# A decoder layer with two attentions: other filler slots, reciprocals copied by ScalarE, an earlier weight split and a deferred normalisation

## The reference

```python
x = layernorm(x + self_attention(x, Wq, Wk, Wv, Wo))          # causal, 16 heads of 32, 4 key/value heads
x = layernorm(x + cross_attention(x, ctx, Wq, Wkv, Wout))      # causal, 16 heads, latent context of 128
x = layernorm(x + ffn(x))                                      # gate, then 2 layers of two matrix products each
```

## Time and profile before

| | |
|---|---|
| Runs, us | 988.43, 987.88, 986.71; median 987.88 |
| Profiled execution, us | 984.96, span 983.1, mean granted TensorE clock 0.971 |
| Busy share of the span | PE 91%, PEld 75%, DVE 69%, ACT 56%, POOL 51% |
| Turn 0 begins (first scores) | 20.8 us |
| Turns 1 to 6 (loop) | 46.5 to 231.3 us |
| Turn 7 | 231.3 to 276.9 us |
| Turn 8 | 276.9 to 332.3 us |
| Turns 9 to 14 | 332.3 to 596.1 us |
| Turn 15 and flush | 596.1 to 653.3 us, where the feed-forward phase has its first TensorE work |

### The profile page before, as it was taken

One profiled execution on the slowest core, in us unless ns is written; L12 is line 12 of the kernel. 1 busy time (PEld: TensorE's weight loads), 2 busy tenths in 40 slices (PEclk: granted clock), 3 DMA queues, 4 the chain that ended last, 5 costly groups with the idle time before them and its releaser, 6 DMA issues. The chain is left out here.

```text
span 983.1 us, 19518 instructions
## 1 busy us (share of the span) xinstructions
PE 892.4 (91%) x5892; PEld 735.8 (75%) x5892; DVE 677.2 (69%) x2055; ACT 550.1 (56%) x1674; POOL 496.7 (51%) x793
## 2 busy tenths in 40 slices
PE   4999999998898899999999998669899999999893
PEld 4888888887776678778777877457678778778672
DVE  4687778786785777777876766426757657667557
ACT  4756556664664566565755556427564464564461
POOL 0445555455755345454645432610665565566466
PEclk9999999999899999999999999879999999999997
DMA  4644243444665556574654636344002001001001
GB/s 155 222 144 158 98 160 128 160 160 143 210 205 145 168 159 194 166 225 121 188 170 138 181 110 197 132 167 155 0 1 85 3 1 55 32 1 40 4 0 43
DMA packets 79075, 118.53 MB, mean 121 GB/s; under 512 B 7920, under 2 KB 41744, under 8 KB 78224
## 3 DMA queue, kind: packets, MB, share of 16 engines
q1 hardware_dynamic: 78992, 117.52, 37.2%
HBM read 58.76 MB, written 17.83 MB: 78 GB/s over the span
## 5 line engine op out<-in xcount | busy, mean ns | idle before, releaser
L920 ACT ACTIVATE prob<-bank,nmax 128x128 f32<-128x128 f32 (+1 forms) x512 | 209.9, 431 | 38.5 <-DVE nmax L1049 36.9
L161 PE MATMUL bank<-w_ffn,hT 128*128 128x512 f32 x768 | 192.8, 402 | 0.0
L1049 DVE CUSTOM_DVE_ANT_0 bank<-bank,mask 128x128 f32<-128x128 f32 (+1 forms) x512 | 167.6, 383 | 4.0 <-PE bank L1225 3.7
L161 PEld LDWEIGHTS bank<-w_ffn,hT 128*128 128x128 f32 x768 | 141.5, 189 | 30.9
L161 PE MATMUL bank<-xT,w_att 128*128 128x256 f32 x864 | 124.1, 298 | 22.0 <-DVE w_att L961 10.3
L161 PEld LDWEIGHTS bank<-xT,w_att 128*128 128x128 f32 x864 | 115.4, 201 | 31.7 <-DVE xT L1037 9.7
L777 POOL TENSOR_TENSOR zone<-raw,zone 128x256 fp32r<-128x256 f32 x128 | 95.2, 776 | 65.8 <-ACT zone L900 65.8
L1237 PE MATMUL bank<-ident,prob 128*128 128x128 f32 x768 | 119.7, 279 | 4.5 <-ACT probT L933 4.4
L933 ACT ACTIVATE probT<-bank 128x512 f32<-128x512 f32 x97 | 58.3, 603 | 92.7 <-PE bank L1261 91.6
L920 ACT ACTIVATION_READ_ACCUMULATOR prob<-bank,nmax 128x1 f32 x512 | 110.0, 215 | 0.0
L1547 ACT ACTIVATE ht<-bank,cols 128x128 f32<-128x128 f32 x192 | 72.3, 457 | 66.0 <-PE bank L1715 66.0
(11 more groups left out here) (118 smaller groups left out, 1518.7 us busy)
## 6 DMA issues: line engine op xcount, KB each, us to landing
q<-stage SPq DMA_DIRECT2D x192, 128.0 KB, 2.2
k<-kstage SPq DMA_DIRECT2D x48, 256.0 KB, 3.5
x<-xres SPq DMA_DIRECT2D x16, 512.0 KB, 4.0
raw<-in_ent_wT SPq DMA_DIRECT2D x32, 256.0 KB, 3.8
raw<-in_ent_pw SPq DMA_DIRECT2D x32, 256.0 KB, 4.1
raw<-in_xT SPq DMA_DIRECT2D x8, 512.0 KB, 3.6
raw<-in_path_w SPq DMA_DIRECT2D x8, 512.0 KB, 3.7
xres<-in_x SPq DMA_DIRECT2D x8, 512.0 KB, 4.9
```

The lines of the kernel that those rows point to most:

```text
L161: ins = t.matmul(out, lhs(a, k), rhs(b, k), start=first and n == 0 and m == 0, stop=last and n == len(kts) - 1 and m == 2, skip_group_chec ...
L920: ins = s.activation(prob[:, u, c * width:(c + 1) * width], banks[u][:, c * width:(c + 1) * width], ACT.Exp, scale=-1.0, bias=nmax[:, i % ...
L1049: ins = v.tensor_tensor_reduce(scored, scored, mask[:, S - width:S], scale=-1.0, scalar=3e38, op0=ALU.add, op1=ALU.min, accum_out=nmax[:, ...
```

## The change

Five things change. First, the slots of a self turn: sv 1 moves from slot 1 to slot 0, wo 0 from slot 2 to slot 1. In turn 8 wo 0 and wo 1 move forward within their slots, in turn 15 cq 3, wout 0 and wout 1 move one slot ahead. Second, the copy rT goes from VectorE to ScalarE, behind the exponentials of unit 0; VectorE's product o now stands behind the maxima of unit 1. Third, in turn 7 the weights of the cross attention are split in slots 0, 1 and 2 (1, 4 and 1 pieces), where they were in slots 0, 1, 2 and 3 (1, 2, 2, 1). Fourth, their pieces are loaded earlier (two already in turn 0), for which they take other places in the parking area. Fifth, a slot's last normalisation stands behind the following step on VectorE, except in the last slot of a turn. GpSimd's split of the next input (`split_x`) goes ahead of the slot's fillers.

```diff
         if own == "self":
-            out[0] += [("sv", 0), ("sq", 2)]
-            out[1] += [("sv", 1), ("sq", 3)]
+            out[0] += [("sv", 0), ("sq", 2), ("sv", 1)]
+            out[1] += [("sq", 3)]
+            if wo:
+                out[1] += [(wo, 0)]
             if after == "self":
+                out[2] += [("sk", 0), ("sq", 0)]
                 if wo:
-                    out[2] += [(wo, 0)]
                     out[3] += [(wo, 1)]
-                out[2] += [("sk", 0), ("sq", 0)]
                 out[3] += [("sq", 1)]
             else:
                 out[1] += [("x1t", 0), ("x1t", 1)]
-                out[2] += [("wo", 0), ("ck", 0), ("cq", 0), ("sp", 0), ("sp", 1)]
+                out[2] += [("ck", 0), ("cq", 0), ("sp", 0), ("sp", 1)]
                 out[3] += [("wo", 1), ("cq", 1), ("ck", 1), ("sp", 2)]
         elif own == "cross" and after:
             out[0] += [U, U, ("cq", 2), U]
             if wo == "wo":
-                out[1] += [U, ("cq", 3), U, ("cv", 0), ("cv", 1), ("x1t", 0), ("x1t", 1), U, ("wo", 0)]
-                out[2] += [U, ("ck", 0), U, ("cq", 0), ("wo", 1)]
+                out[1] += [U, ("cq", 3), U, ("wo", 0), ("cv", 0), ("cv", 1), ("x1t", 0), U, ("x1t", 1)]
+                out[2] += [U, ("wo", 1), ("ck", 0), U, ("cq", 0)]
...
         elif own == "cross":
-            out[0] += [("cq", 2)]
-            out[1] += [("cq", 3), ("cv", 0), ("cv", 1), ("gs", 0), ("gs", 1)]
-            out[2] += [("wout", 0), ("gs", 2), ("gs", 3)]
-            out[3] += [("wout", 1), ("gs", 4), ("gs", 5)]
+            out[0] += [("cq", 2), ("cq", 3)]
+            out[1] += [("cv", 0), ("cv", 1), ("wout", 0), ("gs", 0), ("gs", 1)]
+            out[2] += [("wout", 1), ("gs", 2), ("gs", 3)]
+            out[3] += [("gs", 4), ("gs", 5)]
...
-            return {(0, False): (OUTPUTS, C_KEYS), (1, False): (C_KEYS, C_KEYS + 2), (2, True): (C_KEYS + 2, C_QUERIES),
-                    (3, True): (C_QUERIES, C_VALUES)}.get((i, early), (0, 0))
+            return {(0, False): (OUTPUTS, C_KEYS), (1, False): (C_KEYS, C_QUERIES), (2, False): (C_QUERIES, C_VALUES)}.get((i, early), (0, 0))
...
                 if t is last_self:
-                    load_piece(0)
+                    wait_alone(q, s_wlo, OUTPUTS, s_passed)
+                    load_piece(2)
+                    load_piece(3)
...
                     if i == 2 and t is first:
+                        load_piece(0)
+                        load_piece(1)
...
                         load_path(t)
-                        for n in range(1, 4):
-                            load_piece(n)
+                        wait_alone(q, s_pbm, 2, s_passed)
+                        load_piece(4)
+                        load_piece(5)
...
                         if t.scored(i):
                             exponentials(u)
+                        if u == 0 and t.closed(i):
+                            n = t.groups(i - 2)
+                            s.wait_ge(s_O, n)
+                            if t.before or i > 2:
+                                s.wait_ge(s_o, t.groups(i - 3))
+                            s.activation(rT[:, i % 2, :], banks[O_BANK][:, S:2 * S], ACT.Copy).then_inc(s_rT, 1)
...
                     n = t.groups(i)
-                    v.wait_ge(s_O, n)
                     bank = banks[O_BANK]
-                    v.tensor_copy(rT[:, i % 2, :], bank[:, S:2 * S]).then_inc(s_rT, 1)
                     v.wait_ge(s_rT, n)
...
-                        if u == 0 and t.closed(i):
+                        if u == 1 and t.closed(i):
                             output(i - 2)
...
+                ready = None
                 for i in range(t.steps()):
                     step(i)
+                    if ready:
+                        normalise(*ready)
+                        ready = None
                     weights(*split_at(t, i, True))
-                    ready = None
...
-                    if ready:
+                    if ready and i == t.steps() - 1:
                         normalise(*ready)
```

More of the change, by code:

```diff
@@ L473, in attention_phase @@
     parked = zone_raw[:, 2 * 4 * D:2 * 4 * D + PARKED * D].rearrange("p (n d) -> p n d", n=PARKED)
+    PARKING = [2, 3, 0, 1, 4, 5]
     modb = zone_raw[:, 3 * 4 * D:4 * 4 * D].rearrange("p (n d) -> p n d", n=NL * NP)
@@ L479, in piece_home @@
         if n < PARKED:
-            return parked[:, n, :], s_wring[n], 16
+            return parked[:, PARKING[n], :], s_wring[n], 16
         return x1b[:, n % 2, :], s_wring[PARKED + n % 2], 16 * ((n - PARKED) // 2 + 1)
@@ L664, in between @@
                             q.dma_start(A["fd"][l, 1][:, KT, :], acc[:, NP * l, :]).then_inc(s_pbst, 16)
-                        for n in range(4, PARKED):
-                            load_piece(n)
                         wait_alone(q, s_xs, B, s_passed)
@@ L821, in body @@
                         path_bias(i)
+                    if i == 1 and t.after == "self":
+                        split_x()
                     for name in t.fillers(i):
@@ L828, in body @@
                             gate_lo(name[1])
-                    if i == 1 and t.after == "self":
-                        split_x()
                     if i == 1 and t.after == "cross":
```

## The result

| | before | after |
|---|---|---|
| Runs, us | median 987.88 (986.71 to 991.15, 5 runs) | median 1046.02 (1042.08 to 1052.38, 5 runs) |
| Ratio, 95% interval | | 1.0593 [1.0553, 1.0633] |
| Profiled execution: span, mean granted clock | 983.1, 0.971 | 1050.6, 0.937 |

The change makes the kernel 5.9% slower. The forecast was 1048 us.

The account below looks back on a forecast made before the run. TensorE's work was taken to bound loop and cross turns, with waits in turns 7 and 8. Terms summing to +62.6 us on the profiled 984.96 gave 1047.5, forecast as 1048 us, range 1000 to 1068.

Parts of the forecast that it names:

- (a): Slot 0 of a loop turn: sv 1 waits at least 2.0 us for ScalarE to copy sv 0.
- (b): Each step: rT on ScalarE lengthens the chain; sv 0 is free 6.2 us after the first maxima, against 5.2.
- m: Loop turn: time from its start to VectorE's first maxima, which would grow from 3.0 to 6.0 us.
- The clock: Loop turns: the low clock after a wait of 6 us adds 2.5 us per turn, bounds 0 and 4.
- (c): Slot 1 of a loop turn: wo 0 waits 1.65 us for GpSimd's split of the previous turn's last group.
- the extra DMA in turn 0 (0.5 MB) is hidden: Turn 0: the extra 0.5 MB load costs nothing, since what stands behind it is not needed for 4 us.
- the first: Loop turns: waits alone, m near 3 us, wait 3.0, clock up; turn 33.9 us, kernel about 1015; chance 0.21.
- The faster case: Evened slots hide VectorE if sv 0 is copied within 6.2 us of a turn's start; about 966 us; chance 0.12.

Follow-up runs that it names:

- experiment 6: The changed kernel with wo 0 of the self turns back in slot 2: 1042.2 us, ratio 1.0572 to the kernel before.
- experiment 7: The changed kernel with sv 1 and wo 0 in their old slots and rT back on VectorE: 976.2 us, ratio 0.9884 to before.
- experiment 4: The kernel before with rT copied by ScalarE and o behind the maxima of unit 1: 1020.7 us, ratio 1.0337.
- experiment 3: The kernel before with sv 1 moved to slot 0 of the self turns alone: 999.8 us, ratio 1.012.
- experiment 5: The changed kernel with sv 1 back in slot 1 and rT back on VectorE, wo 0 staying in slot 1: 986.6 us, ratio 0.9983 to before.
- experiment 1: The changed kernel with sv 1 back in slot 1 of the self turns: 1021.8 us, ratio 1.037 to before.
- experiment 8: The changed kernel with GpSimd's path work cut to 32 of 512 columns: 1027.7 us, ratio 1.0411 to before.
- experiment 9: The kernel before with only the early weight pieces and their split over three slots of turn 7: 983.1 us, ratio 0.9953.
- experiment 2: The changed kernel with rT and o back on VectorE at unit 0: 997.4 us, ratio 1.0085 to before.

## Why the prediction was right

By the medians the kernel grew by 58.1 us, and 60 was forecast. Term by term, from the starts of the turns in the two traces:

| Stretch | Forecast | Measured |
|---|---|---|
| Turn 0 | +0.8 | +3.5 |
| Turn 1, turn 2 | +6.0, +7.1 | +6.8, +7.1 |
| Turns 3 to 6 | +36.8 | +35.4 |
| Turn 7 | +4.5 | +2.8 |
| Turn 8 | -3 | -2.3 |
| Turns 9 to 14 | +8.4 | +10.3 |
| Turn 15 and flush | +2 | +0.2 |
| Before turn 0, feed-forward | 0 | +3.8 |
| Sum | 62.6 | 67.5 (span) |

(a) The floor was right: 2.0 us counted, 1.96 to 2.50 us with sv 1 moved alone.

(b) The chain was right to 0.2 us. From the first maxima to o it is 214.17 - 211.13 = 3.04 us (3.15 forecast), from o to the last copy 1.66 (1.7), from there to the end of sv's drain 217.19 - 215.83 = 1.36 (1.4). By itself this edit costs more than the other two together (3.4%, against 1.2% for sv 1 and 0.2 or 1.0% for wo 0 in experiments 6 and 7). The prediction did not say so: in a loop turn it followed the chain only into the waits for sv and wo, and in experiment 4 the chain costs 3.4% where neither product has moved. That it left this out did no harm here, because in after the wait of sv 1 covers them: the waits for exponentials and probT copies in turns 2 to 6 come to 13.0 us in experiment 4 and to 2.2 in after.

The size that was off is m, the time from the turn's start to its first maxima: 5.2 us in turn 5 and 4.5 to 5.2 in turns 2 to 7, instead of 6.0. The part up to step 3 held (its maxima 2.7 us into the step in turn 4, 2.75 forecast). But the step with its slot took 8.3 us instead of 7.6, so the next turn began 0.7 us later and found VectorE so much further on. The sv wait is therefore 4.1 to 4.9 us in turns 2 to 7, not 6.0.

The clock made up for it. In turn 5 the slow stretch costs 2.82 - 1.54 = 1.3 us in sv. The next step lasts from 219.87 to 225.70, 5.8 us instead of 3.3. Together that is 3.8 us, where 2.5 was taken and 4 was the upper bound. For turn 5 the old turn of 30.2 us, the sv wait of 4.9, the clock's 3.8, the wo 0 wait of 0.9 and a probT wait of 0.4, less the old wait of 0.6, give 39.6 us. Forecast were 39.4, measured 39.8 in this turn and 38.4 to 39.8 over the loop. That the number is so close is luck: the sv wait was taken a microsecond too long and the clock's cost about as much too small.

The Trainium skill, "TensorE: Matmul & The Clock Gate", section "HAM oscillation — how this bites in real kernels", describes a loop that waits in every pass and pays the low level in every pass. In after the trace agrees in every loop turn (mean clock 0.87 to 0.91). In experiment 3, where the wait is half as long, the rows fall to the low level in five of seven turns.

(c) wo 0 waits 0.6 to 1.5 us, forecast 1.65. The low clock stretches the step before it for both sides. In turn 5 the o of step 1 comes at 6.4 us of the step instead of 4.6, and TensorE is there at 7.5 us instead of 4.8; the second grew more, so the wait is 0.9. The 1.0% between experiments 5 and 7 is no measure of this term, since wo 0 waits for sv 1's bank there.

Turn 0 is the one step that was wrong in kind: "the extra DMA in turn 0 (0.5 MB) is hidden". The next score needs a query stack, whose landing shares the DMA engines with the 0.5 MB and with the 1 MB of path bias. Between 40 and 55 us the copies of 128 KB to the query stacks land in 3.3 us in after, 2.3 before (2.5 to 4.6 us in the eight kernels with these loads, with wide scatter). Turn 1 begins with 2.69 us of waiting for q, 1.43 before: 1.3 of the 3.5 us. Another 1.9 us have arisen before step 3 of turn 0, where TensorE stays at the low level until some 34 us, in before until 28.5. Whether the change did that is open: over those eight kernels turn 0 takes 25.7 to 31.1 us, and it took 25.7 before.

The growth of turns 9 to 14 is the chain's for 8.7 us; the rest is in turn 9, which takes 47.5 us in after and 45.9 to 46.0 in experiments 1, 4, 6 and 8. The other +3.8: 0.6 us ahead of turn 0 and 3.2 us in the feed-forward phase, whose work is unchanged (1412 matmuls in both), at a mean clock of 0.96 instead of 0.97. The traces show that this is not the change's. Over the fourteen profiled executions that phase takes 329.7 to 329.9 us in six, 331.4 to 331.5 in two and 332.9 to 333.2 in six. Experiments 1, 6 and 8, which keep most of the change, have 329.7 to 329.8; experiment 9, which has none of the costly edits, has 333.0. The profiled execution was also 7.3 us above the mean of the other four runs of after (1052.38 against 1045.04).

The rivals: the first (waits alone, clock up, 1015) had m and the wait too small. Experiment 8, where most of `path` is gone, has its small m (2.4 to 3.1 us) and a wait below its 3.0, but turns of 35.8 to 36.9 us instead of 33.9, at a clock of 0.91 to 0.95: there the clock does not stay up. The faster case needed sv 0 copied at 6.2 us of a turn; it was at 11.2.

## What to carry to other kernels

Before a product is moved into a slot as its third, ask who drains the bank of the first and what stands ahead of that on its engine; it happened twice here, to sv 1 in after and to wo 0 in experiment 5. A copy that VectorE has time for is not free on ScalarE when it lands between two links of a chain that TensorE waits for: a copy of 0.4 us per step, taken off an engine that was 79% busy in a loop turn, made the kernel 33 us slower. And a change of five edits should be timed edit by edit: here three edits cost 7.2% (1.0593 / 0.9884) and the rest gained 1.2%.

## What the runs showed of the hardware

I had not expected how unevenly TensorE's clock answers to a wait. These are rows of sv 1 and of what follows it in experiment 3 (timeline of TensorE, turns 2, 5 and 6); the products ahead of each wait had run at full speed:

```profile
90.28 2.61 PE L161 MATMUL bank<-w_att,xT 128*128 128x128 f32 x12 [1.97 <-ACT sv L859]
92.68 1.05 PE L1225 MATMUL bank<-k,q 96*128 96x128 f32 x4
...
191.16 1.55 PE L161 MATMUL bank<-w_att,xT 128*128 128x128 f32 x12 [2.34 <-ACT sv L859]
192.56 0.68 PE L1225 MATMUL bank<-k,q 96*128 96x128 f32 x4
193.03 1.08 PE L1237 MATMUL bank<-ident,prob 128*128 128x128 f32 x4
...
224.06 1.55 PE L161 MATMUL bank<-w_att,xT 128*128 128x128 f32 x12 [1.97 <-ACT sv L859]
225.45 0.61 PE L1225 MATMUL bank<-k,q 96*128 96x128 f32 x4
225.90 0.62 PE L1237 MATMUL bank<-ident,prob 128*128 128x128 f32 x4
```

The product takes 1.54 us at 2.4 GHz. After a wait of 1.97 us it takes 2.61 us in turn 2 and the rows behind it are at the low level (1.2 GHz); after the same 1.97 us it takes 1.55 us in turn 6, and nothing behind it is slow. The turns last 34.3 and 31.3 us. In turn 5, after 2.34 us, the product itself is at full speed and the fall comes two microseconds later, in the transposes (1.08 us instead of 0.62); that turn lasts 33.3 us. Experiment 2 has a slow stretch behind a wait of 1.67 us and none behind waits of 2.35 and 2.39. In after, with waits of 4.1 to 4.9 us, all six turns have the slow stretch; in five the product takes 2.8 us, in one 1.98, with low rows behind it. So the cost of a wait of about 2 us in a loop cannot be told from its length, it differs from turn to turn of one execution, and the product right behind the wait does not show it: the rows of the whole next step have to be read.
